# Other places for the scatters and the gathers in GpSimd's order of work (macaron block with routed experts and dilated attention, one core)

## The reference

```
x = x + 0.5 * ffn(layernorm(x))
x = x + attn(layernorm(x))
x = x + 0.5 * ffn(layernorm(x))

ffn(x):   q, k, v = split(x @ w_qkv)              # 16 heads of 8
          o = softmax(causal(q k^T / sqrt(8))) v   # inside each sequence
          h = layernorm(x + o @ w_o) * g1 + b1
          the two best of 8 experts for each token, by h @ wg, with weights that sum to 1
          y = sum over the two of weight * (gelu(h @ w1[e] + bb1[e]) @ w2[e] + bb2[e])
          return layernorm(h + y) * g2 + b2
```

## Time and profile before

| | |
|---|---|
| median of 3 runs | 1053.31 us (1052.3 to 1055.62) |
| span of the profiled execution, first to last instruction | 1192.8 us |
| PE busy in it | 1022.4 us, 86% |
| DVE, ACT, POOL busy | 680.8, 670.5, 572.7 us (57%, 56%, 48%) |
| POOL's selects L1173 | 256, 182.5 us |
| POOL's scatters L1222 and gathers L1236 | 128 and 128, 124.5 and 123.7 us |
| mean granted clock of PE in it | 0.898 of 2.4 GHz |

### The profile page before, as it was taken

The page is one execution under the profiler, slowest core; times in us unless marked ns, Lnnn a source line. Parts: engine busy times, 40 slices in busy tenths (PEclk is TensorE's granted clock), DMA queues, the critical chain, the costliest instruction groups (busy, mean ns, idle before and its releaser), DMA issues. The chain is left out here.

```text
span 1192.8 us, 29724 instructions
## 1 busy us (share of the span) xinstructions
PE 1022.4 (86%) x10913; PEld 818.6 (69%) x10913; DVE 680.8 (57%) x2458; ACT 670.5 (56%) x1494; POOL 572.7 (48%) x693
## 2 busy tenths in 40 slices
PE   4799979998989989999989989998999988866470
PEld 2566656886877867686777867687777866766470
DVE  5657665655558835686568835686556723520314
ACT  1243424875758756675667757576666756534240
POOL 2223356235465455555565455554464456542515
PEclk9988877998999989898999979799999979887795
DMA  3394105555555545555556545555556545676562
GB/s 71 86 193 109 37 19 162 167 164 181 154 160 150 172 138 156 147 154 172 149 154 171 165 137 144 153 158 154 160 163 176 170 137 164 202 244 221 212 194 51
DMA packets 117239, 181.01 MB, mean 152 GB/s; under 512 B 13128, under 2 KB 80232, under 8 KB 117096
## 3 DMA queue, kind: packets, MB, share of 16 engines
q1 hardware_dynamic: 108904, 162.32, 47.7%
q0 software_dynamic: 8192, 16.79, 4.9%
HBM read 145.10 MB, written 38.68 MB: 154 GB/s over the span
## 5 line engine op out<-in xcount | busy, mean ns | idle before, releaser
L1173 POOL TENSOR_SCALAR_AFFINE_SELECT probs<-probs 128x512 f32<-128x512 f32 x256 | 182.5, 721 | 262.1 <-ACT probs L706 257.1
L706 ACT ACTIVATE probs<-ps_quad 128x768 f32<-128x768 f32 x256 | 193.7, 807 | 150.3 <-PE ps_quad L527 87.8
L744 ACT ACTIVATE act<-ps_ring,weights 128x128 f32<-128x128 f32 x696 | 191.8, 387 | 96.4 <-PE ps_ring L623 48.0
L874 DVE TENSOR_REDUCE shift_cols<-ps_quad 128x2 f32<-128x512 f32 (+3 forms) x256 | 149.9, 586 | 139.8 <-PE ps_quad L508 125.6
L632 PE MATMUL ps_ring<-weights,act 128*128 128x128 f32 x1392 | 190.8, 285 | 31.1 <-issue 16.4
L632 PEld LDWEIGHTS ps_ring<-weights,act 128*128 128x128 f32 x1392 | 174.5, 198 | 35.1 <-issue 21.6
L623 PE MATMUL ps_ring<-tile_t,weights 128*128 128x128 f32 x1392 | 187.6, 292 | 3.9 <-issue 3.2
L623 PEld LDWEIGHTS ps_ring<-tile_t,weights 128*128 128x128 f32 x1392 | 174.0, 204 | 16.8 <-issue 13.2
L1236 POOL DMA_INDIRECT picked<-sorted_outputs,place x128 | 123.7, 966 | 79.8 <-issue 78.6
L999 DVE TENSOR_TENSOR tile_y<-ps_ring,weights 128x128 f32<-128x128 f32 x174 | 48.8, 287 | 182.2 <-PE ps_ring L632 101.2
L1222 POOL DMA_INDIRECT sorted_rows<-h_rows,place x128 | 124.5, 972 | 53.5 <-issue 34.6
(11 more groups left out here) (165 smaller groups left out, 1531.5 us busy)
## 6 DMA issues: line engine op xcount, KB each, us to landing
weights<-expert_weights SPq DMA_DIRECT2D x174, 578.0 KB
tile_rows<-sorted_rows SPq DMA_DIRECT2D x56, 192.0 KB
sorted_outputs<-tile_y SPq DMA_DIRECT2D x56, 192.0 KB
query_key_parts<-qk SPq DMA_DIRECT2D x32, 256.0 KB, 5.0
k<-query_key_parts SPq DMA_DIRECT2D x64, 64.0 KB
q<-query_key_parts SPq DMA_DIRECT2D x64, 64.0 KB
sorted_rows<-zeros SPq DMA_DIRECT2D x2, 1472.0 KB, 10.7
xs<-in_L_attn_x SPq DMA_DIRECT2D x32, 64.0 KB, 2.3
```

Source lines behind the costliest of these rows:

```text
L706: sc.activation(probs[:, r % PROBS, 2 * a:2 * a + 2, :], ps_quad[:, 2 * a:2 * a + 2, 0:3 * P], ACT.Exp, scale=HD ** -0.5).then_inc(pair_fr ...
L744: ins = sc.activation(act[:, k % ACTS, f, :], bank(use)[:, f * P:(f + 1) * P], ACT.Gelu_apprx_tanh, bias=weights_of(k)[:, 2 * F + f:2 * F ...
L874: dve.tensor_reduce(shift_cols[:, late, groups], ps_quad[:, groups, 0:split], AX.X, ALU.max)
L1173: pool.affine_select(out=both, in_=both, compare_op=ALU.is_ge, fill=0.0, base=0, pattern=[[0, 2], [0, 2], [1, P]], channel_multiplier=-1). ...
```

## The change

Six numbers of the table change. `scatter1` moves from 11.917 to 12.45, `scatter2` from 12.578 to 13.0, `scatter3` from 13.235 to 13.5; `gather0` from 22.948 to 22.6, `gather1` from 23.074 to 23.1, `gather2` from 23.31 to 23.4. `scatter0`, `gather3` and everything else stay. The order of PE, DVE, ACT and SP is the same as before, instruction by instruction; only POOL's differs.

```diff
-    "turn_mid": 6.856, "route": 7.124, "gate": 7.191, "rank": 11.86, "scatter0": 11.876, "scatter1": 11.917,
-    "scatter2": 12.578, "scatter3": 13.235, "load_tiles0": 13.754, "load_tiles": 12.816, "load_weights0": 13.277,
+    "turn_mid": 6.856, "route": 7.124, "gate": 7.191, "rank": 11.86, "scatter0": 11.876, "scatter1": 12.45,
+    "scatter2": 13.0, "scatter3": 13.5, "load_tiles0": 13.754, "load_tiles": 12.816, "load_weights0": 13.277,
...
-    "store_tiles": 15.433, "gather0": 22.948, "gather1": 23.074, "gather2": 23.31, "gather3": 23.765,
+    "store_tiles": 15.433, "gather0": 22.6, "gather1": 23.1, "gather2": 23.4, "gather3": 23.765,
```

## The result

The changed kernel takes 1076.21 us (median of four, 1070.73 to 1079.57) where the kernel before takes 1052.80 us (median of four, the three of the table above and one of 1047.11): 1.0242 of it, 95% interval 1.0191 to 1.0294. It is slower by some 23 us. I had forecast 1054.5, from 1026 to 1066.

What follows compares the result with a forecast made beforehand. PE was taken to set the pace, with the slow stretches behind indirect DMAs put down to the profiler. All terms were 0 but +1.3 us for the moved scatters, on 1053.31: 1054.5 us, range 1026 to 1066.

Steps and rivals of the forecast that it cites:

- PE sets the pace, and a clean odd sequence takes 28.5 us: Sequences during which POOL issues no indirect DMA: PE is busy nearly throughout; the odd one takes 28.50 us with 363 matmuls.
- Are the stretches in the timed runs?: Slowdowns of all engines but POOL behind rows of indirect DMAs, 24.1 us a set: taken as the profiler's, timed runs nearly free.
- the span "near 1150 while the time doesn't move": Sign of being right: the profiled span falls 20 to 70 us below 1192.8, though the time doesn't fall.
- Row of eight cut in two, gain 0: Eight scatters split on POOL: next group's selects come 5 us earlier, but PE waits for no select, so gain 0.
- Last four scatters one group later, +1.3 us (0 to some 4): Scatters ahead of `residual` and `rstd`: covers of 1.1 and 1.3 us, late only in set 6; +1.3 us.
- The wait forecast for the last such set: Set 6, DVE's step waiting for POOL's `rstd` behind the moved scatters: 2.6 us late.
- `gather0` behind the last store, 0: POOL's first gathers of a set stand one group earlier, behind the last store; no cost counted for it.
- Row of six ahead of `rstd`, "hidden by 1.1 us": Six gathers on POOL behind the third group's selects take 7.6 us; `rstd` ends at 483.7, DVE uses it at 484.83.
- What lateness costs: Set 6: half of DVE's 2.6 us lateness was taken for PE, 1.3 us, bounds 0 and 2.6.
- POOL comes late at several places: Rival: issuing ahead of an `rstd` that DVE awaits, twice a set, costs 7 to 25 us, likely 9 (1062); chance 0.21.
- The slow stretches are real: Rival: timed runs have the stretches, so the change gains 21 to 71 us (1008), chance 0.14; in part (1032 to 1049), 0.12.
- The change doesn't do what it says: Rival: despite four transfers at most between selects, one row of six stays per set; changes nothing in the forecast; no own chance.

## Why the prediction was wrong, step by step

**PE sets the pace, and a clean odd sequence takes 28.5 us**: right at both levels, 28.50 with 363 or 364 matmuls.

**Are the stretches in the timed runs?** The answer (no) was right for the timed runs by luck: its reason (the profiler's writing) was wrong, and the sum that I leaned on, 6 x 24.1 against 139.5 us, fits just as well when trace and times are of two levels. Of the two things that could differ between a profile of 1192.8 and times of 1053, profiling and chip, I considered only the first. Where a run has both a time and a span, the time is 1.8 us longer: 1056.58 against 1054.8, 1203.48 against 1201.7, 1079.57 against 1077.8. I had put aside the statement of the Trainium skill ("Runtime: NRT & Kernel Launch", section "The ~15µs preamble/postamble breakdown") that a profile's total and the execution time differ by about the same 6.2 us whatever the kernel. The runs agree that there is a small gap that doesn't change with the kernel; theirs is another one, from the first to the last instruction, so the 6.2 us are neither found nor refuted here. So of the signs that I named, the span "near 1150 while the time doesn't move" couldn't come: span and time are one thing.

**Row of eight cut in two, gain 0**: right at the 1053-level. No stretch is behind any row there, and the scatter sequence is 28.70 us in both kernels.

**Last four scatters one group later, +1.3 us (0 to some 4)**: the signs came as forecast. The mid norm's `rstd` ends at 420.17 where it ended at 416.72, with DVE's step at 420.31, and the selects of group 3 end at 421.38 with their use at 422.19: covers of 0.1 and 0.8 us, forecast 1.1 and 1.3. The wait forecast for the last such set, 2.6 us, is there with 3.2. SP's first load of set 2 stands at 420.0 instead of 414.7, and a late load reaches PE once, 8.2 us against 5.9 before. Measured alone the part costs 4.8 us, between 2.1 and 8.5: the sign right, the size short. Where the rest of it lies no trace shows.

**`gather0` behind the last store, 0**: too low. Alone it costs 3.9 us (1.5 to 6.2); 0.8 of them lie in the five sequences, and where the rest lies isn't shown. The cover that I named didn't exist either. SP issues the last store at 424.32 and POOL's first gather leaves at 431.40, so by POOL's wait it landed up to 7.1 us after its issue, not 2. POOL stood 5.49 us for it. PE's only wait for a select of more than 0.3 us, 2.75, is in the first set, so the distance from the selects to `weigh` covered it, not the order of store and gather. And this edit had a second effect that I didn't price by itself: it puts the odd job's first gathers ahead of the norm's `rstd`.

**Row of six ahead of `rstd`, "hidden by 1.1 us"**: this is the step that failed. The length of the row was right: forecast 7.6 us, measured 438.93 to 446.65, 7.7. The distance that had to cover it was not. I took it from the earlier trace rows, 475.02 (end of the selects) to 484.83 (DVE's step), 9.8 us. The same distance in the kernel before at the 1053-level is 438.20 to 445.18, 7.0 us; after, DVE was ready at 447.84 - 2.25 = 445.59, 6.8 us behind the selects. The 2.8 us between come from a slow stretch: the earlier trace rows lie behind a row of six, in a sequence that was 6.3 us too long by my own reckoning, and the granted clock there is at half. The trace of the prediction, over the time of these selects:

```profile
472.00:478.00 6.00, 6.00 (x51) 4.42 (x52) 4.31 (x27) 2.68 (x6) 3.19 (x4) 0.50 0.46 143
```

In the kernel before at the 1053-level PE makes 96 matmuls in the same place (434 to 440 us), at a granted clock of 1.00. I had just argued that the timed runs don't have these stretches, and then measured covers inside them. From the end of the selects to the end of `rstd` it is 9.0 us (438.77 to 447.73): 0.8 hidden at the distance with the stretch in it, 2.2 late at the one without. At the 1200-level no row of six makes DVE wait, but not by my sum: a new slow stretch stands inside the distance, which is 13.7 us in set 2 (468.77 to 482.47).

**What lateness costs.** For set 6 I took half of DVE's lateness for PE. Here 2.25 us on DVE became 2.70 on PE and 4.2 in the end, since DVE's next steps ran into POOL's selects (0.55 and 1.13 us longer) and the granted clock fell behind the gap (1.4 us). The share was a half in the forecast and is nearly 2.

**The rivals.** "POOL comes late at several places" is what happened, and at the point that I gave for it: it decides, I wrote, if the pace between select and use is over 1.1 us shorter than in the trace. It is 2.8 us shorter. I priced it at 7 to 25 us, likely 9, and it took 23.4; with 0.21 for it and a likeliest value near its low end, the range stopped at 1066. "The slow stretches are real" is right as well, at the 1200-level: but even there the change gains nothing that can be told (0.9981), where I had given 21 to 71 us for it. Its price took 5.5 us a set for the scatters, and their six sequences gain 3.0 in all, since rows of four lose time too; it took 3.1 to 6.3 us a set for the gathers, and what the third sequences gain (26.0 us) the second ones mostly give back (18.2). "The change doesn't do what it says" was right as a description, and that row of six is what costs most.

## What to carry to other kernels

A profile and a median can come from different conditions, here two levels of speed. When they are 13% apart, look for what the difference is before taking any distance from the trace, and if a part of the trace isn't in the timed runs, then the slack measured across that part isn't either: recompute each cover at the pace of the undisturbed stretches. In a queue that issues one by one (1.25 to 1.27 us a transfer on POOL) list all deadlines behind the moved row, here `rstd` of one norm, `rstd` of the next, and the landing for the combine, since taking a row away from one puts it on another. A gap of PE can cost its length and the clock behind it (here 2.70 us and 1.4).

## What the runs showed of the hardware

- Two levels of one kernel, 1053 and 1186 to 1201 us, single runs within 1.1% of the median of their occasion. At the higher one PE, DVE and ACT nearly stop from some 5 us into a row of indirect transfers issued back to back (13 matmuls in 5 us in the row of eight), while POOL goes on at its rate; behind rows of four it is there too (PE busy 0.54 of the 2 us from 432 in the changed kernel, 4.19 of the 6 us from 440). At the lower one there is nothing of it. What makes the one level or the other isn't known.
- A store issued at 424.32, among loads (DMA share 0.81 in that sequence), had landed by 431.40, up to 7.1 us later, where the last store of the program took 1.99. A gather landed at most 2.0 us after the end of its issue (450.04 to 452.02).
- DVE and POOL drag out each other's instructions when they meet: 1310 ns instead of 335 for a 128x128 step of DVE, 2.33 us instead of 1.42 for two selects, depending on which began first.
